# Sorting edges into windows with the edge data stationary, magnitudes from squares on ScalarE, and the unrolled branch first, in a two-block graph network on one core

## The reference, cut to what matters

```python
def layer(x, rows, cols, vals, W, b):             # twice; rows = src, cols = dst
    neigh = segment_sum(vals[:, None] * x[cols], rows, num_segments=N)
    return relu(concatenate([x, neigh], axis=1) @ W.T + b)
x = layernorm(x + layer(layer(x, ..., W0, b0), ..., W1, b1))
h_sparse = maxk(x @ W_neigh, 32)                  # the 32 largest of each row
neigh = segment_sum(h_sparse[src], dst) / maximum(deg, 1)
x = layernorm(x + x @ W_self + neigh)
```

## Time and profile before

| | |
|---|---|
| median of three runs | 713.2 us (710.86 to 713.54) |
| the profiled execution | 714.56 us, of which the span of instructions is 712.8 us |
| PE, DVE, ACT, POOL busy | 641.9, 512.7, 341.1, 109.8 us |
| DMA | 73.09 MB |

### The profile page before, as it was taken

One profiled execution on the slowest core, in us unless ns is written; L12 is line 12 of the kernel. 1 busy time (PEld: TensorE's weight loads), 2 busy tenths in 40 slices (PEclk: granted clock), 3 DMA queues, 4 the chain that ended last, 5 costly groups with the idle time before them and its releaser, 6 DMA issues.

```text
span 712.8 us, 11318 instructions
## 1 busy us (share of the span) xinstructions
PE 641.9 (90%) x3987; PEld 347.3 (49%) x3988; DVE 512.7 (72%) x1306; ACT 341.1 (48%) x657; POOL 109.8 (15%) x190
## 2 busy tenths in 40 slices
PE   4918788888887999999999999999999979999996
PEld 3717566666643444444444444444444434444443
DVE  6579988999937787888885467878778853734433
ACT  4318878999947576777765233333333320100000
POOL 4000222222210001010110122232323200000000
PEclk9999999999998999999999999999999999999999
DMA  9413454545540011111110366555554504310000
GB/s 212 85 45 97 149 177 152 164 155 159 156 148 22 29 39 35 39 34 43 31 44 23 109 177 186 154 182 167 167 177 154 166 18 138 116 54 24 22 25 27
DMA packets 39543, 73.09 MB, mean 103 GB/s; under 512 B 3120, under 2 KB 32207, under 8 KB 39481
## 3 DMA queue, kind: packets, MB, share of 16 engines
q1 hardware_dynamic: 39481, 72.30, 34.1%
HBM read 38.91 MB, written 33.38 MB: 101 GB/s over the span
## 4 chain that ended last, share of the span: by engine, by line
PE 70%; DVE 19%; ACT 4%; DMA 3%; issue 2%; SPq 1%; POOL 0%; DVEq 0%; ACTq 0%; POOLq 0%
PE pair L1510 35%; PE bank L1600 9%; PE pair L1600 8%; DVE hots L632 7%; PE bank L1400 7%; PE pair L1400 4%; PE bank L1392 2%; DVE ct L775 2%; ACT own L1083 2%; PE pair L1293 2%; DVE x_t L768 1%; PE bank L1406 1%; DMA w_nat<-in_L_gnn_W_dram 1%; DMA own_in<-own_dram 1%; ACT x_t L1076 1%
## 5 line engine op out<-in xcount | busy, mean ns | idle before, releaser
L1510 PE MATMUL pair<-xs,ct 125*128 125x512 f16 x625 | 147.1, 387 | 0.0
L1510 PE MATMUL pair<-a,ct 125*128 125x512 f16 x625 | 142.8, 379 | 0.0
L632 DVE TENSOR_TENSOR hots<-iota,jobs 128x1792 f16<-128x1792 f16 (+1 forms) x100 | 104.2, 1061 | 4.6 <-issue 3.9
L1510 PEld LDWEIGHTS pair<-xs,ct 125*128 125x128 f16 x625 | 62.2, 101 | 70.9 <-issue 5.7
L1510 PEld LDWEIGHTS pair<-a,ct 125*128 125x128 f16 x625 | 61.0, 99 | 68.1
L1065 ACT ACTIVATE slab<-pair 125x875 f16<-125x875 f32 (+1 forms) x100 | 83.7, 861 | 20.5 <-PE pair L1369 19.1
L1187 ACT ACTIVATE a<-ct 125x1000 f16<-125x1000 f16 (+1 forms) x75 | 80.2, 1069 | 8.4 <-DMA c_dram<-slab 7.5
L1600 PE MATMUL bank<-xs,ct 125*128 125x512 f16 (+1 forms) x325 | 71.5, 379 | 0.0
L1600 PE MATMUL pair<-xs,ct 125*128 125x512 f16 x300 | 66.4, 379 | 0.0
L1369 PE MATMUL pair<-hots 128*128 128x125 f16 x625 | 54.2, 228 | 12.4 <-ACT slab L1065 7.4
L1392 PE MATMUL bank<-ident,slab 125*128 125x125 f16 x625 | 52.6, 223 | 12.9 <-DVE ct L775 10.9
(11 more groups left out here) (199 smaller groups left out, 859.6 us busy)
## 6 DMA issues: line engine op xcount, KB each, us to landing
c_dram<-slab SPq DMA_DIRECT2D x25, 683.6 KB
ct<-c_dram SPq DMA_DIRECT2D x25, 683.6 KB
own_in<-own_dram SPq DMA_DIRECT2D x50, 125.0 KB
own_dram<-own SPq DMA_DIRECT2D x25, 125.0 KB
own_dram<-own_st SPq DMA_DIRECT2D x25, 125.0 KB
x_in<-in_x_dram SPq DMA_DIRECT2D x25, 125.0 KB
z_dram<-z_st SPq DMA_DIRECT2D x25, 125.0 KB
a<-z_dram SPq DMA_DIRECT2D x5, 625.0 KB
```

What stands on the lines that cost most here:

```text
L632: v.tensor_tensor(hots[k][:, :, :, :].rearrange("p w g (a d) -> p (w g) a d", d=2), iota, job, ALU.is_equal).then_inc(win_hot, 1)
L1510: ins = mm(agg[k % 3][0:lhs.shape[1], :], lhs, parts[l][:, t, :], start=t == 0, stop=t == NT - 1, skip_group_check=True)
```

## The change

1. **Picks.** The edge data is stationary (128 columns of `quint` or `piece`), and `pick` moves, 320 and 305 windows at a time. The result has edges in partitions and windows in the free dimension, which is what `jobs` needs, so the transposes (L1303) and the copies out of their PSUM banks are gone. `PICKS` has two parts, for which 52 matmuls are issued, 4 of them heads. ScalarE writes all of `jobs` from SBUF (`jobs_out`).
2. **Magnitudes.** VectorE's maxima of absolute values are gone. ScalarE squares the same data with a running sum (`square_x`, `square_weights`) and takes roots (`roots`, a Sqrt, for which its function table is loaded anew). Two of the four `square_x` stand ahead of the read of `matched`, the others among the slab copies of t = 0.
3. **Order.** VectorE makes three of the four sets of hots of t = 0 ahead of `matched`, and the fourth right behind it. The steps of the scales move back: `bounds_t` behind `transposes(0, ., 1)` of t = 1, `bounds_row` behind `fill(1, 3)`, `scales_b` behind `fill(2, 0)`. On VectorE `bounds` stands in t = 1 ahead of the first `ct` copy. `w_high(0)` and `w_high(1)` move to t = 2.
4. **Branch.** The unrolled path stands first in the program, the general path behind it.

```diff
-PICKS = [(0, 2), (2, 4), (4, 5)]
+PICKS = [(0, 320), (320, QN)]
...
-                            last = mm(out, pick[:, g, i * P:(i + 1) * P], m[:, g * P:(g + 2) * P],
+                            last = mm(out, m[:, at:at + 128], pick[:, g, lo:hi],
                                       start=False, stop=g == EQ - 1 and n == 2, skip_group_check=True)
...
-                        last = nc.tensor.transpose(b[:, at:at + P], m[:, i, :], identf[0:P, 0:P])
...
+            def square_x(c):
+                act.wait_ge(x_loaded[c], BOTH)
+                if c:
+                    act.wait_ge(squared, c)
+                n = (XC[c + 1] - XC[c]) * F
+                a.activation(slab[1][:, 0:n], xs32[:, XC[c]:XC[c + 1], :].rearrange("p t f -> p (t f)"), ACT.Square, scale=TINY,
+                             accum_out=squares[0:P, c:c + 1]).then_inc(squared, 1)
...
+            def roots():
+                act.wait_ge(squared, 7)
+                a.activation(norms[:, :], squares[:, :], ACT.Sqrt).then_inc(rooted, 1)
+                act.wait_ge(rooted, 1)
+                a.activation(stat[:, 0:4], norms[:, 0:4], ACT.Copy, scale=1.0 / TINY).then_inc(stat_ready, 1)
+                a.activation(stat[:, 10:16], norms[:, 4:10], ACT.Copy, scale=1.0 / TINY).then_inc(stat_ready, 1)
...
+            slots_out(0)
+            jobs_out(0)
+            slots_out(1)
+            jobs_out(1)
             for l in range(2):
                 for h in range(2):
                     weights_out(l, h)
+            act.wait_ge(act_step, 4)
+            act.wait_ge(const_ready, 17)
+            square_x(0)
+            square_x(1)
...
             total = pe.value_load(matched[0:1, 0:1], min_val=0, max_val=E)
+            with pe.If(total > E - 1):
+                fills()
             with pe.If(total < E):
                 general_table()
...
-            with pe.If(total > E - 1):
-                fills()
```

More of the change, by code:

```diff
@@ L793, in _ @@
             total = dve.value_load(matched[0:1, 0:1], min_val=0, max_val=E)
+            with dve.If(total > E - 1):
+                quick_hots(1, 0)
+                clear_tr()
+                for k in range(1, FILLS):
+                    quick_hots(1, k)
+                bound_rows()
+                for t in range(1, NT):
+                    more, own = t + 1 < NT, OWN[t]
+                    if more:
+                        quick_hots(t + 1, 0)
+                    if t == 1:
+                        bounds()
+                    tr_copy(t - 1, 1)
+                    if 1 < t < 5:
+                        w_low(2 * t - 4)
+                    if more:
+                        quick_hots(t + 1, 1)
+                    if t == 1:
+                        scales_out()
+                    if 1 < t < 5:
+                        w_low(2 * t - 3)
+                    if t == 2:
+                        own_low(0)
+                    if own and own[0] + 1 < NT:
+                        own_low(own[0] + 1)
+                    if more:
+                        quick_hots(t + 1, 2)
+                        quick_hots(t + 1, 3)
+                    tr_copy(t - 1, 3)
+                    if len(own) > 1:
+                        own_low(own[1] + 1)
+                for g in (1, 3):
+                    tr_copy(NT - 1, g)
             with dve.If(total < E):
@@ L1095, in quick_copies @@
             def quick_copies():
-                for f in range(FILLS):
-                    quick_copy(0, f)
+                quick_copy(0, 0)
+                square_x(2)
+                quick_copy(0, 1)
+                square_x(3)
+                quick_copy(0, 2)
+                square_weights()
+                roots()
+                quick_copy(0, 3)
                 for t in range(1, NT):
@@ L1103, in quick_copies @@
                     tr_copy(t - 1, 0)
+                    if t == 2:
+                        ready_for_own()
+                        w_high(0)
+                        w_high(1)
                     quick_copy(t, 1)
@@ L1446, in fills @@
             def fills():
-                for f in range(2):
+                for f in range(FILLS):
                     fill(0, f)
-                bounds_t()
-                for f in range(2, FILLS):
-                    fill(0, f)
-                bounds_row()
-                scales_b()
                 pe.wait_ge(tr_cleared, 2)
@@ L1458, in fills @@
                     fill(t, 0)
+                    if t == 2:
+                        scales_b()
                     if own:
@@ L1463, in fills @@
                     transposes(t - 1, par, 1)
+                    if t == 1:
+                        bounds_t()
                     if own:
```

237 lines of the change are left out of this document (96 added, 141 removed).

## The result

The changed kernel takes 718.88 us (median of 8 runs), the kernel before 711.55 us (median of 8 runs beside them): a ratio of 1.0095, with a 95% interval of 1.0054 to 1.0135. On the 713.2 us from which I forecast that is 6.8 us more, with an interval of about 2.9 us on either side. The forecast was 6.8 us, 720.0. The total is right. In the traces its two large terms are off in opposite directions, so that the agreement is this close is luck.

What follows compares the result with a forecast made beforehand. DVE's queue was taken to bound the rebuilt 40 to 60 us, PE stage 2. Terms 2.5 + 3.9 + 0.4 = 6.8 us on the 713.2 us median gave 720.0 us, own range 717 to 723, wider range 714.5 to 723.5.

Steps and rivals of the forecast that it cites:

- Picks: Prelude: regrouped pick matmuls take 15.0 against 15.4 us, the longer last part takes back the gain; next to nothing.
- Start of stage 1: First slabs of stage 1: ScalarE's squares and later scale steps make DVE wait 7.0 us; 2.5 us lost, from 1.0 to 4.5.
- End of stage 1: Before the first aggregation: the taken branch stalls PE uncovered, +3.9 us, from 0 to 5.5; DVE's and ACT's stalls hidden.
- the clock: End of stage 1: PE's clock drop may last longer after the added pause; +0.4 us, between 0 and +1.7.
- (2): End of stage 1: the late branch costs nothing because its target has been fetched; 715.7 us, chance 0.10.
- (3, 4): Picks: clock rises in their second half, 716 us, chance 0.10; or near the first pick, 709.4 us, chance 0.08.
- rival 4: Picks: clock rises near the first pick, picks take 7.2 instead of 15.0 us; 709.4 us in total, chance 0.08.

Runs made afterwards that it cites:

- d2: Kernel before with only the new picks, `jobs` written by ScalarE; maxima, order and branches as before: 0.9987 of the kernel before.
- b1: Kernel before with only the unrolled path put first on PE, ACT and DVE: 1.0051 of the kernel before.
- a3: Changed kernel without the general path and the second test of `matched` on all engines: 1.0015 of the kernel before.
- a1: Changed kernel with the general path first again on PE, ACT and DVE: 1.0060 of the kernel before.
- e1: Changed kernel with scales early, general path first on PE alone, that branch brought into PE's idle time: 0.9903 of the kernel before (703.03 us).

## Why the prediction was right, step by step

**Picks, forecast 0.** Held. A group of 13 matmuls takes 3.69 and 3.53 us from start to start, where I had 3.84 and 3.67: my fixed part was 0.15 too large. The last `jobs` copy ends at 32.1 us instead of 33.6, mostly because I had the picks start as in the profiled execution before, in which the weights came late: 14.38 for their first matmul. Here the first pick is at 13.75, and its head was done before. Alone the part gives 0.9987.

**Start of stage 1, forecast +2.5.** The mechanism is the one described: squares between slab copies (1.76 and 1.57 us with their reads, forecast 1.86 and 1.64), the table load 1.28, and a wait of 6.94 us for `stat_psum`, forecast 7.0 (from the forecast's own times, 45.3 to 52.6, it is 7.3). But the term was mis-sized: every time in the chain is 1.5 to 2.5 us earlier than forecast (`stat_psum` read at 50.4 instead of 52.6, the `ct` copy ending at 60.6 instead of 63.1), and at t = 6 the changed kernel is level and not 2.5 us behind. Being level is itself an accident of the execution that I compared with, whose prelude was 1.7 us late. At t = 6 the copy is 1.6 us behind that of d2 (97.44), and 1.8 behind that of b1 (94.38) with the 2.84 us of VectorE's stall added. So by the traces the term is between 1 and 2 us. By the ratios it is a3's, +1.0 us (-0.6 to 2.7), made up of -3.8 for leaving the general path out of the kernel before (b2) and +4.8 for parts 1 to 3. The forecast of 2.5 is inside that interval, and the sign is not clear of noise. By the Trainium skill (ScalarE: Activation LUTs, "What ACT_TABLE_LOAD costs") the load would have cost 1.4 us more with its drain; the trace does not agree, since the root starts 1.29 us behind the start of the load.

**End of stage 1, forecast +3.9 and +0.4 for the clock.** The stall is on PE where it was put, uncovered, and those of DVE and ACT are hidden, as said. Its size was wrong: 5.97 us for the branch, 5.61 idle, above my upper end of 5.5. I took the early branch's duration for one at the end of stage 1; why that is longer is not shown. The clock took 1.1 us more of the first 50 matmuls than before, forecast 0.4. (The 1.7 us that I gave for one drop fits: 12.56 us before, 10.96 in a1, a3 and d2, which had none. It does not follow from 12 matmuls instead of 17, which would be 1.0.) By the runs, changed against a3, the late branch costs 5.7 with its clock in it, good to 3.3. The rule of the Trainium skill (Runtime: NRT & Kernel Launch, "Instruction fetch mechanics"), that a taken branch to code outside the part fetched ahead has to wait for it, agrees with 5.61, 7.06 and 5.80 us of idle time in three kernels; it gives no price.

**Sum.** Forecast 2.5 + 3.9 + 0.4 = 6.8. By the runs 1.0 + 5.7 = 6.7. That this meets the measured 6.8 proves nothing, since the pieces are the steps from before to a3 and from a3 to changed, which add up by construction. Against them the start was 1.5 too high and the end 1.4 too low, each less than its interval. What the traces say of the two errors is firmer: about 1 us too high at the start, and at the end 5.61 + 1.1 = 6.7 where I had 4.3. Together they make some 8 us, more than the measured 6.8 but within its interval.

**Rivals.** A late branch that costs nothing (2) is refuted by the 5.61 us. A clock that rises in the picks (3, 4) did not happen in the profiled execution: matmuls of 320 columns follow each other at 0.27 us, which is 1.2 GHz, to the end of the picks. It can happen. In a3, with the same prelude, the first picks run at twice that speed, for about 1 us, and then no longer:

```profile
13.65 0.43 PE L1294 MATMUL pair<-pick,piece 100*128 100x320 f16 x2
...
15.15 0.74 PE L1294 MATMUL pair<-pick,piece 100*128 100x320 f16 x2
```

The cast of `matched` is 1.2 us earlier there than in the changed kernel, 0.2 of it from an earlier start. e1's picks begin in the same way. So the start of rival 4 is seen, and not its size. Of the eight runs of the changed kernel one took 711.82 us; it has no trace, and whether its clock rose and stayed up is not known. By its fills (six in 0.84 us at 57.99, in 0.50 at 66.54) PE of the changed kernel was at its lower level until 65.95 us, before until 59.9. VectorE's `bounds` left it nearly empty (busy 0.16 of 3.4 us), and then the granted clock was 0.50 for 10.25 us. Little was lost by that: from t = 0 to 1 the `ct` copies are 6.71 us apart, before 6.43.

## What to carry to other kernels

Work that is taken off the full engine gains nothing if its replacement stands in the queue of an engine that the full one waits for: 6.3 us of VectorE's maxima became a wait of 6.94 us, and the same squares moved into ScalarE's waits in the prelude gave 4.0 us, with the steps behind them moved up as well 7.6. A taken branch has to be placed on each engine by itself, where that engine waits anyway: early on PE and late on VectorE and ScalarE was 0.55% better than late on all three; early on all three (1.0060 against 1.0040) is not told apart from it. Before a term is worked out against one profiled execution, compare its early landmarks with those of other executions of the same code.

## What the runs showed of the hardware that was not expected

- A taken branch on PE over the general path took 3.34 to 3.80 us at 33 to 37 us, with DMA nearly still, and 4.69 to 7.28 us at the end of stage 1. VectorE's cost 2.84 us early and 7.24 to 7.61 late.
- In a1, where the path that holds the Sqrt stands ahead of the unrolled path in ScalarE's text, the unrolled path begins with a table load of 1.28 us, although the Sqrt was never executed. In the changed kernel, where it stands behind, there is no load at that place.
- A running sum costs ScalarE a read of 0.19 us behind every square, and the square itself takes 1.48 us for 1536 values and 1.69 for 1792.
